# A DRAM buffer re-laid by head: one load over 96 partitions where there were six over 16

## The chip, the cores and the metric

The kernel runs on one core of one Trainium2 chip. The metric is the device time of one execution in microseconds (us), from the start of the program to its end. It does a whole transformer-like block for 32 batches of 512 tokens with hidden size 256: a token mixing, an attention with relative position terms, and a mixture of 8 experts.

## The reference, cut to what matters

The reference computes `h = tok(x)`, then `h = h + attn(layernorm(h))`, then `h = h + ffn(layernorm(h))`. The change touches only the attention's queries and keys:

```python
q = _split_heads(hidden_states @ Wq + bq, b, s)          # 16 heads of 16
k = _split_heads(hidden_states @ Wk + bk, b, s)
scores = jnp.einsum('bhqd,bhkd->bhqk', q, k) / scale
pos_k = (re @ Wpk + bpk) ...; pos_q = (re @ Wpq + bpq) ...
c2p = take_along_axis(einsum('bhqd,hpd->bhqp', q, pos_k), c2p_idx) / scale
p2c = swapaxes(take_along_axis(einsum('bhkd,hpd->bhkp', k, pos_q), p2c_idx)) / scale
probs = softmax(scores + c2p + p2c)
ctx = einsum('bhqk,bhkd->bhqd', probs, v); return ctx @ Wo + bo
```

## The kernel before, in words

The program runs in stages one after the other: a short table stage, `project`, `attend`, `output`, `choose`, `experts`. The change touches the DMA instructions of `project` and of `attend`, both issued by SyncE (SP).

**Splitting a number in three.** Queries and keys are float32, but the matmuls of the scores run in bfloat16. So `project` splits each value into three bfloat16 parts (high, middle, low), and the product of two such values is taken as six products of parts (`SLOTS = 6`, with `SIDE_A` and `SIDE_B` naming the part of each side). For one head of 16 features the contraction is therefore over `ST = 6 x 16 = 96` rows, and three more rows carry a term of the keys. These 99 rows are the `stack` of a head: 96 (or 99) partitions by `SW = 1280` columns, of which 512 are queries and 768 keys.

**project** (lines 313 to 634) works batch by batch, 32 times. In one batch TensorE mixes the tokens (`mixing`, line 394), turns the normalised rows, and makes queries, keys and values; ScalarE and GpSimd and VectorE keep and split them into `part_q` and `part_k`, tiles of 128 partitions (8 heads of 16 features), 2 halves `c` (heads 0 to 7 and 8 to 15) and 512 or 768 columns, three parts each. `part_q` and `part_k` have two buffers, `xt` (the input) has two, `v_sb` has one. SP's program for one batch `n`, in this order (lines 358 to 377): wait until the mixing of `n` has been done and load the input `xt` of batch `n + 2`; store `d_h`; wait for the values and store `d_v`; wait for all parts, and write them into `d_stack` in DRAM with 12 transfers (`for j in range(SLOTS)`, one of queries and one of keys each); write `d_kterm` with two. ScalarE waits for the writes of two batches ago before it fills `part_q` and `part_k` again, and for the `d_kterm` writes of the batch before.

**attend** (lines 636 to 1033) works head by head, 512 heads in all, numbered `n`; a loop runs over the batches and a Python `for` over their 16 heads. For head `n + 5` TensorE makes the position tables (`tables`, line 847) from `stack`, ScalarE keeps them in `skew_in`, and SP writes them to DRAM (`write_tables`, line 730) and reads them back, two heads later, at another pitch (`read_tables`, line 740), which is how the take-along-axis is done. GpSimd and VectorE finish the table of a head (`part`, `fill`), TensorE adds it to the head's scores in PSUM (`scores`, lines 860 to 867), VectorE moves the scores out, adds more table and takes the maximum (line 999), TensorE turns them (`turn`, line 876), ScalarE takes the exponent, and TensorE makes the context (line 889).

The stack of two heads (a group) is one buffer of a ring of `SR = 4`. SP loads group `k + 3` at head `2k`, after `read_tables(n + 3)` in program order: it waits until the scores of the group that had the buffer are done, and issues six loads of 16 partitions by 2 heads by 1280 columns from `d_stack` (line 714) and one of three partitions from `d_kterm` (line 717). After them come `write_tables(n + 5)`, and at some heads loads of the values (line 721) and a store of the context (line 746). TensorE needs the group for `tables` of head `2k + 6`, which it does during head `2k + 1`; its wait there is on all seven transfers (`STACKS = SLOTS + 1`), and everything that TensorE has behind it in program order waits too.

**output** (from line 1035) reads the context and the softmax sums back, with transfers whose DRAM side is `[8, 16, 512]` and whose SBUF side is 128 partitions (`load_inputs`, `load_shares`), and GpSimd multiplies them (line 1145).

Of the kernel before, what the change touches and what calls it, by code (L numbers as in the profile page):

```python
# [17 lines left out]
BF16 = mybir.dt.bfloat16  # L18
# [6 lines left out]
P = 128  # L25
S = 512
H = 256
ND = 4
NH = 16
HD = H // NH  # L30
QT = S // P
HC = H // P
# [17 lines left out]
SLOTS = 6  # L50
SIDE_A = (0, 0, 1, 0, 2, 1)
SIDE_B = (0, 1, 0, 2, 0, 1)
ST = SLOTS * HD
PLAIN = 3
KW = S + S // 2
SW = S + KW
# [4 lines left out]
SH = 2  # L61
# [10 lines left out]
def after(eng, sem, count):  # L72

    if not isinstance(count, int) or count > 0:
        eng.wait_ge(sem, count)  # L75


def settled(eng, sem, count, passed):


    after(eng, sem, count)
    if not isinstance(count, int):
        eng.sem_inc(passed, 1)  # L83


def peeled(eng, steps, body):

    body(0, steps == 1)
    if steps > 2:
        with eng.Fori(1, steps - 1, 1) as i:  # L90
            body(i, False)
    if steps > 1:
        body(steps - 1, True)


def build(nc, io, B):
    T = B * S
    NT = T // P
    with ExitStack() as top:
        def sem(name):  # L100
            return top.enter_context(nc.semaphore(name))

        def dram(name, shape, dt=F32):
            return nc.dram_tensor(name, shape, dt).ap()

        passed = sem("passed")
        d_tab = dram("d_tab", (2, 3, H, TW), BF16)
        d_stack = dram("d_stack", (B, SLOTS, H, SW), BF16)
        d_plain = dram("d_plain", (PLAIN, NH, TW), BF16)
        d_kterm = dram("d_kterm", (B, 3, NH, KW), BF16)  # L110
        d_v = dram("d_v", (B, S, NH * VROW))
        d_h = dram("d_h", (B, S, H))
        d_skew = dram("d_skew", (RING, P, PITCH))
        d_ctx = dram("d_ctx", (B, NG, P, S))
        d_share = dram("d_share", (B, NH, S))
        d_xg = dram("d_xg", (T, XG))
        d_scores = dram("d_scores", (P, NE, NT))
        d_floor = dram("d_floor", (P, 2))

        with ExitStack() as ctx:  # L120
            project(nc, io, B, ctx, sem, passed, d_tab, d_plain, d_stack, d_kterm, d_v, d_h)
        with ExitStack() as ctx:
            attend(nc, io, B, ctx, sem, passed, d_tab, d_plain, d_stack, d_kterm, d_v, d_skew, d_ctx)
        with ExitStack() as ctx:
            scores = ctx.enter_context(nc.sbuf_tensor("scores", [P, NE, NT], F32))
            with ExitStack() as inner:
                output(nc, io, B, inner, sem, passed, scores, d_h, d_ctx, d_share, d_xg)
            chosen = ctx.enter_context(nc.sbuf_tensor("chosen", [P, NE, CT], U32))

            w1, w2, b2 = (ctx.enter_context(nc.sbuf_tensor(name, shape, F32)) for name, shape in (  # L130
                ("w1", [P, 2, HC, DFF]), ("w2", [P, 2, FC, H]), ("b2", [P, 2, H])))
            w_in = [sem(f"e_w_in{u}") for u in range(2)]

            def load_expert(sp, e, u):
                sp.dma_start(w1[:, u], io["w1"][e].rearrange("(c p) f -> p c f", p=P)).then_inc(w_in[u], 16)
                sp.dma_start(w2[:, u], io["w2"][e].rearrange("(c p) o -> p c o", p=P)).then_inc(w_in[u], 16)
                sp.dma_start(b2[:, u], io["b2"][e].partition_broadcast(P)).then_inc(w_in[u], 16)

            with ExitStack() as inner:
                choose(nc, io, NT, inner, sem, passed, scores, chosen, d_scores, d_floor, load_expert)  # L140
            with ExitStack() as inner:
                experts(nc, io, T, inner, sem, passed, chosen, d_xg, w1, w2, b2, w_in, load_expert)


def project(nc, io, B, ctx, sem, passed, d_tab, d_plain, d_stack, d_kterm, d_v, d_h):
    def sb(name, shape, dt=F32):
        return ctx.enter_context(nc.sbuf_tensor("p_" + name, shape, dt))
# [17 lines left out]
    with ExitStack() as tctx:  # L165
# [47 lines left out]
        with nc.Block() as block:  # L213
            @block.sync
            def _(sp):
                for dst, src in loads:
                    sp.dma_start(dst[:], src).then_inc(t_in, 16)
                for u in range(2):

                    sp.dma_start(xt[:, u], xT[u].rearrange("d (c p) s -> p (d c) s", p=P)).then_inc(x_in[u], 16)  # L220
                sp.wait_ge(t_dve, 26)
                for w in range(2):
                    for c in range(HC):
                        sp.dma_start(d_tab[w, :, c * P:(c + 1) * P, :].rearrange("t p x -> p t x"),
                                     parts[:, w, c]).then_inc(t_out, 16)
                sp.dma_start(d_plain.rearrange("t h x -> h t x"), plain_parts[:]).then_inc(t_out, 16)
                sp.wait_ge(t_out, 16 * (2 * HC + 1))
# [104 lines left out]
    part_q = sb("part_q", [P, 2, 3, HC, S], BF16)  # L332
    part_k = sb("part_k", [P, 2, 3, HC, KW], BF16)
# [14 lines left out]
    h_out = [sem(f"p_h_out{u}") for u in range(2)]  # L348
    v_out, t_out = sem("p_v_out"), sem("p_t_out")
    parts_out = [sem(f"p_parts_out{u}") for u in range(2)]  # L350
    DMAS = 2 * SLOTS
    CH = 2 * HC
    pairs = B // 2

    with nc.Block() as block:
        @block.sync
        def _(sp):
            def body(i, last):
                for u in range(2):
                    n = 2 * i + u  # L360
                    if not last:
                        settled(sp, h_done, 2 * (n + 1), passed)
                        sp.dma_start(xt[:, u], xT[n + 2].rearrange("d (c p) s -> p (d c) s", p=P)
                                     ).then_inc(x_in[u], 16)
                    settled(sp, h_kept, 2 * (n + 1), passed)
                    sp.dma_start(d_h[n].rearrange("(t p) o -> p t o", p=P), h_sb[:, u]).then_inc(h_out[u], 16)
                    settled(sp, v_kept, 2 * (n + 1), passed)
                    sp.dma_start(d_v[n].rearrange("(t p) o -> p t o", p=P),
                                 v_sb[:].rearrange("p t h r -> p t (h r)")).then_inc(v_out, 16)
                    settled(sp, parts_done, (CH + 1) * (n + 1), passed)  # L370
                    for j in range(SLOTS):
                        to = d_stack[n, j].rearrange("(c p) x -> p c x", p=P)
                        sp.dma_start(to[:, :, 0:S], part_q[:, u, SIDE_A[j]]).then_inc(parts_out[u], 16)
                        sp.dma_start(to[:, :, S:SW], part_k[:, u, SIDE_B[j]]).then_inc(parts_out[u], 16)
                    to = d_kterm[n].rearrange("t h x -> h t x")
                    sp.dma_start(to[:, :, 0:S], part_t[0:NH]).then_inc(t_out, 16)
                    sp.dma_start(to[:, :, S:], part_t[NH:, :, 0:KW - S]).then_inc(t_out, 16)

            peeled(sp, pairs, body)
            sp.wait_ge(v_out, 16 * B)  # L380
            sp.wait_ge(t_out, 32 * B)
            for u in range(2):
                sp.wait_ge(parts_out[u], 16 * DMAS * pairs)
                sp.wait_ge(h_out[u], 16 * pairs)
# [75 lines left out]
        def _(act):  # L460
# [13 lines left out]
            def keep_qk(n, i, u, m):  # L474
                c = m % HC
                if m == 0:
                    after(act, parts_out[u], 16 * DMAS * i)
                if m == HC:
# [157 lines left out]
def attend(nc, io, B, ctx, sem, passed, d_tab, d_plain, d_stack, d_kterm, d_v, d_skew, d_ctx):  # L636
    def sb(name, shape, dt=F32):
        return ctx.enter_context(nc.sbuf_tensor("a_" + name, shape, dt))

    def ps(name, shape, dt=F32):  # L640
# [7 lines left out]
    stack = sb("stack", [ST + 3 + PLAIN, SR, SH, SW], BF16)  # L648
# [16 lines left out]
    stack_in = [sem(f"a_stack_in{u}") for u in range(SR)]  # L665
# [4 lines left out]
     pv_done, ctx_kept, ctx_out) = (sem("a_" + n) for n in (  # L670
         "tab_done", "tab_kept", "high_kept", "parted", "filled", "s_done", "s_kept", "lowered",
         "turn_done", "turned", "pv_done", "ctx_kept", "ctx_out"))
    STACKS = SLOTS + 1
    HEADS = B * NH
    PARTS = 5
    TURN = 2
# [21 lines left out]
    with nc.Block() as block:  # L698
        @block.sync
        def _(sp):  # L700
# [9 lines left out]

            def load_stack(b, g):
                u = g % SR
                for j in range(SLOTS):
                    sp.dma_start(stack[j * HD:(j + 1) * HD, u],
                                 d_stack[b, j, g * SH * HD:(g + 1) * SH * HD].rearrange("(h d) x -> d h x", d=HD)
                                 ).then_inc(stack_in[u], 16)
                sp.dma_start(stack[ST:ST + 3, u, :, S:], d_kterm[b, :, g * SH:(g + 1) * SH]
                             ).then_inc(stack_in[u], 16)

# [29 lines left out]
            for g in range(SR - 1):  # L749
                load_stack(0, g)  # L750
# [86 lines left out]
        def _(pe):  # L837
            def tables(n, b, hh, part):

                g, w, half = hh // SH, part % 2, part // 2  # L840
                if hh % SH == 0 and part == 0:
                    after(pe, stack_in[g % SR], 16 * STACKS * (NS // SR * b + g // SR + 1))
                after(pe, tab_kept, 4 * n + part - 1)
# [862 lines left out]
```

## Time and profile before

| | |
|---|---|
| Time, median of 3 runs | 5799.73 us (5794.48 to 5809.27) |
| The profiled execution, its time | 5817.07 us |
| Its span in the trace | 5815.3 us |
| TensorE busy | 4793.1 us (82%) |
| VectorE busy | 3453.9 us (59%) |
| ScalarE busy | 2652.2 us (46%) |
| GpSimd busy | 1528.6 us (26%) |
| Moved by DMA | 1543.71 MB, mean 265 GB/s |
| Packets of SP's DMA queue, share of the 16 DMA engines' span | 78.8% |

The stages can be told apart by their lines: `project` runs to 982 us (the last `d_stack` write is issued at 977.4 us), `attend` from there to about 4910 us, `output` to about 5320 us, the experts after it. Most of the time is `attend`. A share of busy time is a mean over all stages, so each stage has to be read by itself.

### The profile page before, as it was taken

To read this page: it belongs to the slowest core of one execution; us is meant where nothing else is said; L and a number is where in the kernel's file an instruction comes from. 1 tells how busy PE (TensorE), PEld (TensorE's weight loads), DVE (VectorE), ACT (ScalarE), POOL (GpSimd) and SP (SyncE) were. 2 spreads that over 40 slices of the span, in tenths; PEclk is the share of its full clock that TensorE was granted. 3 is DMA by queue.
4 is the path that set the end of the run, shared out by engine and by line. 5 is a ranking of instruction groups with operands and counts; after the bars stand their busy time and mean duration, and the time that the engine had idled before them with its cause. 6 is when DMAs were issued, how large, how long until landed. Compare 5 with 4: busy or idle time off the path is not lost. (4 is left out here: it accounts for less than half of the span.)

```text
span 5815.3 us, 116776 instructions
## 1 busy us (share of the span) xinstructions
PE 4793.1 (82%) x31272; PEld 3401.2 (58%) x31272; DVE 3453.9 (59%) x9058; ACT 2652.2 (46%) x4937; POOL 1528.6 (26%) x3442
## 2 busy tenths in 40 slices
PE   6999996788888888888888888888888888774588
PEld 5666664555555655555556555555555555563455
DVE  3344443666666666666667666666666666676611
ACT  1333332555555555555555555555555555010011
POOL 1222232222222222222222222222222222452022
PEclk9999998899999999999999999999999999786589
DMA  4777777999988999998899989999899897674033
GB/s 157 258 254 248 256 258 225 317 313 305 308 299 294 307 310 305 303 311 300 299 309 308 316 296 307 306 304 301 299 305 314 297 301 250 226 253 144 2 78 74
DMA packets 682097, 1543.71 MB, mean 265 GB/s; under 512 B 59715, under 2 KB 300275, under 8 KB 681587
## 3 DMA queue, kind: packets, MB, share of 16 engines
q1 hardware_dynamic: 675446, 1528.58, 78.8%
q0 software_dynamic: 6144, 8.52, 0.9%
q8 instruction: 300, 4.92, 0.4%
q14 instruction: 207, 1.70, 0.1%
HBM read 762.99 MB, written 773.87 MB: 264 GB/s over the span
## 5 line engine op out<-in xcount | busy, mean ns | idle before, releaser
L999 DVE CUSTOM_DVE_ANT_1 a_scored<-a_ps_m_s,a_bias 128x512 f32<-128x512 f32 x2048 | 1398.8, 683 | 1264.7 <-PE a_ps_m_s L867 1238.8
L936 ACT ACTIVATE a_probsT<-a_ps_m_t 128x512 f32<-128x512 f32 x2048 | 1225.7, 605 | 1255.4 <-PE a_ps_m_t L876 1253.1
L815 POOL TENSOR_SCALAR_AFFINE_SELECT a_bias<-a_bias 128x128 f32<-128x128 f32 (+2 forms) x2560 | 903.9, 381 | 2877.8 <-DMA a_bias<-d_skew 2796.8
L930 ACT ACTIVATE a_skew_in<-a_ps_m_tab 128x512 f32<-128x512 f32 x2048 | 1119.4, 608 | 453.7 <-PE a_ps_m_tab L847 392.3
L876 PE MATMUL a_ps_m_t<-a_ident,a_scored 128*128 128x128 f32 x8192 | 1311.3, 285 | 0.5 <-ACT a_probsT L936 0.5
L876 PEld LDWEIGHTS a_ps_m_t<-a_ident,a_scored 128*128 128x128 f32 x8192 | 978.4, 146 | 457.4 <-DVE a_scored L1006 380.2
L847 PE MATMUL a_ps_m_tab<-a_tabs,a_stack 96*128 96x256 bf16 (+1 forms) x4096 | 728.8, 291 | 464.9 <-DMA a_stack<-d_kterm 445.3
L1006 DVE TENSOR_SCALAR a_scored<-a_scored,a_top_of 128x512 f32<-128x512 f32 x2048 | 964.9, 492 | 0.0
L867 PE MATMUL a_ps_m_s<-a_ident,a_bias 128*128 128x128 f32 x5120 | 943.0, 283 | 0.0
L862 PE MATMUL a_ps_m_s<-a_stack 99*128 99x512 bf16 (+2 forms) x2048 | 728.0, 355 | 198.9 <-issue 147.2
L867 PEld LDWEIGHTS a_ps_m_s<-a_ident,a_bias 128*128 128x128 f32 x5120 | 712.9, 148 | 121.9 <-issue 15.4
L847 PEld LDWEIGHTS a_ps_m_tab<-a_tabs,a_stack 96*128 96x128 bf16 (+1 forms) x4096 | 361.8, 103 | 665.0 <-issue 467.1
L889 PE MATMUL a_ps_m_ctx<-a_probsT,a_values 128*17 128x512 f32 x4096 | 563.2, 623 | 1.2 <-ACT a_ctx_sb L942 1.2
L984 DVE COPY_PREDICATED a_bias<-a_ps_m_past,a_high 128x384 f32<-128x384 int32 x1024 | 544.5, 586 | 32.4 <-POOL a_high L801 32.4
L394 PE MATMUL p_ps_m_h<-p_mix,p_xt 128*128 128x256 f32 x2048 | 467.1, 382 | 7.3 <-PEq L213 7.3
L394 PEld LDWEIGHTS p_ps_m_h<-p_mix,p_xt 128*128 128x128 f32 x2048 | 389.9, 192 | 99.6 <-issue 51.9
L862 PEld LDWEIGHTS a_ps_m_s<-a_stack 99*128 99x128 bf16 x2048 | 206.5, 101 | 315.0 <-issue 242.6
L860 PE MATMUL a_ps_m_s<-a_stack 99*128 99x128 bf16 (+1 forms) x1024 | 263.1, 257 | 0.0
L1179 PE MATMUL o_ps_m_o<-o_wo,o_ctxn 128*128 128x256 f32 x512 | 169.3, 503 | 65.3 <-POOL o_ctxn L1145 65.3
L1179 PEld LDWEIGHTS o_ps_m_o<-o_wo,o_ctxn 128*128 128x128 f32 x512 | 130.6, 261 | 94.9 <-POOL o_ctxn L1145 37.2
L539 POOL TENSOR_TENSOR p_rest_q<-p_full_q,p_part_q 128x512 f32<-128x512 f32 x64 | 90.3, 1411 | 330.8 <-ACT p_part_q L486 330.8
L539 POOL TENSOR_TENSOR p_rest_k<-p_full_k,p_part_k 128x768 f32<-128x768 f32 x64 | 105.1, 1643 | 241.5 <-ACT p_part_k L491 241.5
(182 smaller groups left out, 3631.1 us busy)
## 6 DMA issues: line engine op xcount, KB each, us to landing
d_skew<-a_skew_in SPq DMA_DIRECT2D x512, 1024.0 KB, 5.9
a_bias<-d_skew SPq DMA_DIRECT2D x512, 896.0 KB, 7.9
a_stack<-d_stack SPq DMA_DIRECT2D x1536, 80.0 KB
d_stack<-p_part_k SPq DMA_DIRECT2D x192, 384.0 KB, 3.8
p_xt<-in_xT SPq DMA_DIRECT2D x32, 2048.0 KB, 9.4
d_stack<-p_part_q SPq DMA_DIRECT2D x192, 256.0 KB, 3.5
d_ctx<-a_ctx_sb SPq DMA_DIRECT2D x128, 256.0 KB, 6.9
d_v<-p_v_sb SPq DMA_DIRECT2D x32, 544.0 KB, 3.0
```

The source lines that it names most:

```text
L394: mm = pe.matmul(m_h[:, t], xt[:, u, k, t * P:(t + 1) * P], mix[:, k], start=(k == 0), stop=(k == ND * HC - 1))
L815: nc.gpsimd.affine_select(blocks(r + out[0], (out[1], count)), blocks(r + of, (2, count)), pattern=[[0, count], [-sign, P]], base=0, chann ...
L847: mm = pe.matmul(m_tab[:, w, k], stack[0:rows, g % SR, hh % SH, at:at + P], tabs[0:rows, w, hh], start=True, stop=True)
L862: pe.matmul(bank[:, far:], q, row[:, S + far:2 * S], start=not far, stop=False, skip_group_check=True)
L867: mm = pe.matmul(bank[:, k * P:(k + 1) * P], bias[:, at], ident[:], start=False, stop=(k == near[-1]), is_transpose=True, skip_group_check ...
L876: mm = pe.transpose(m_t[:, k % 2, t * P:(t + 1) * P], scored[:, hh % SCORED, t, k * P:(k + 1) * P], ident[:])
L889: mm = pe.matmul(m_ctx[j * CROW:j * CROW + VROW], values[:, half, k, (g * GH + j) % (NH // 2)], turned_at(g, j, k), start=(k == 0), stop=( ...
L930: nc.scalar.activation(skew_in[:, u, w, 2 * half:2 * half + 2], m_tab[:, w], ACT.Identity).then_inc(tab_kept, 1)
L936: nc.scalar.activation(turned_at(hh // GH, hh % GH, k), m_t[:, k % 2], ACT.Exp, scale=SCALE).then_inc(turned, 1)
L984: nc.vector.copy_predicated(blocks(r + at, (step, QT - 1)), m_past[:, w].unsqueeze(1).to_broadcast([P, QT - 1, P]), high[:, v, w].unsqueez ...
L999: nc.vector.tensor_tensor_reduce(split(scored[:, hh % SCORED, t]), split(m_s[:, t % 2]), extra, 1.0, -3.0e38, ALU.add, ALU.max, top_of[:, ...
L1006: nc.vector.tensor_scalar(at, at, top_of[:, hh % 2, t:t + 1], None, ALU.subtract).then_inc(lowered, 1)
```

## The change

In DRAM the stack was laid out `(batch, slot, feature row of all heads, column)`. Now it is laid out `(batch, head, row of the head's 96, column)`. The load of a group becomes one transfer over 96 partitions; the three-row load from `d_kterm` stays, so the wait counts two transfers where it counted seven. The writes in `project` must now say which head a row belongs to, so each covers one half `c` of the heads, and there are 24 per batch where there were 12. The bytes are the same in both directions. The ring keeps its four buffers.

```diff
-        d_stack = dram("d_stack", (B, SLOTS, H, SW), BF16)
+        d_stack = dram("d_stack", (B, NH, ST, SW), BF16)
@@ project
-    DMAS = 2 * SLOTS
+    DMAS = 2 * SLOTS * HC
@@
                     for j in range(SLOTS):
-                        to = d_stack[n, j].rearrange("(c p) x -> p c x", p=P)
-                        sp.dma_start(to[:, :, 0:S], part_q[:, u, SIDE_A[j]]).then_inc(parts_out[u], 16)
-                        sp.dma_start(to[:, :, S:SW], part_k[:, u, SIDE_B[j]]).then_inc(parts_out[u], 16)
+                        for c in range(HC):
+                            to = d_stack[n, c * NH // HC:(c + 1) * NH // HC, j * HD:(j + 1) * HD]
+                            sp.dma_start(to[:, :, 0:S], part_q[:, u, SIDE_A[j], c]).then_inc(parts_out[u], 16)
+                            sp.dma_start(to[:, :, S:SW], part_k[:, u, SIDE_B[j], c]).then_inc(parts_out[u], 16)
@@ attend
-    STACKS = SLOTS + 1
+    STACKS = 2
@@
             def load_stack(b, g):
                 u = g % SR
-                for j in range(SLOTS):
-                    sp.dma_start(stack[j * HD:(j + 1) * HD, u],
-                                 d_stack[b, j, g * SH * HD:(g + 1) * SH * HD].rearrange("(h d) x -> d h x", d=HD)
-                                 ).then_inc(stack_in[u], 16)
+                sp.dma_start(stack[0:ST, u], d_stack[b, g * SH:(g + 1) * SH].rearrange("h r x -> r h x")
+                             ).then_inc(stack_in[u], 16)
                 sp.dma_start(stack[ST:ST + 3, u, :, S:], d_kterm[b, :, g * SH:(g + 1) * SH]
                              ).then_inc(stack_in[u], 16)
```

Before, the two sides of a write were `[128, 2, 512]` on both sides; now the DRAM side is `[8, 16, 512]` (8 heads, 16 rows of each) and the SBUF side `[128, 512]`.

## Rows read from the trace of the kernel before

**Rows 1.** Windows of project, attend, output: busy us (instructions) by engine, clock, DMA.

```profile
core 0: us, PE busy (x) PEld busy (x) DVE busy (x) ACT busy (x) POOL busy (x), PEclk, DMA share, GB/s
150.00:900.00 750.00, 726.29 (x2873) 509.73 (x2872) 305.14 (x696) 252.82 (x450) 219.28 (x160) 1.00 0.76 254
1100.00:4800.00 3700.00, 3116.19 (x23258) 2175.59 (x23256) 2487.64 (x6786) 2131.32 (x3998) 943.05 (x2905) 0.94 0.92 305
5000.00:5300.00 300.00, 235.72 (x1147) 198.51 (x1148) 230.06 (x607) 38.13 (x87) 159.88 (x85) 0.82 0.72 246
```

**Rows 2.** Waits of PE, 1050:4950: us in total, times, longest.

```profile
PE a_ps_m_tab L847 <- DMA a_stack<-d_kterm: 402.7, 221, 4.2
PE a_ps_m_s L862 <- issue: 147.2, 29, 5.6
```

**Rows 3.** Timeline of SP in attend, heads 2k, 2k+1, 2k+2: start, duration.

```profile
3072.35 0.52 SPq L740 DMA_DIRECT2D a_bias<-d_skew  x1
3073.12 2.92 SPq L714 DMA_DIRECT2D a_stack<-d_stack  x6
3076.22 0.25 SPq L717 DMA_DIRECT2D a_stack<-d_kterm  x1
3078.76 0.52 SPq L740 DMA_DIRECT2D a_bias<-d_skew  x1
...
3086.35 0.79 SPq L740 DMA_DIRECT2D a_bias<-d_skew  x1
```

**Rows 4.** Timeline of PE in the same heads, in brackets the idle time before.

```profile
3081.24 0.61 PE L847 MATMUL a_ps_m_tab<-a_tabs,a_stack 96*128 96x256 bf16 x4 [1.28 <-DMA a_stack<-d_kterm]
```

**Rows 5.** Source view of the table reads of all 512 heads, line 740.

```profile
L740 SPq DMA_DIRECT2D a_bias<-d_skew x512: 518/524/1736, 1015.7 to 4897.4; - x171
```

**Rows 6.** Windows of 4 us: stack load flowing, not flowing, after a long stall.

```profile
3076.00:3080.00 4.00, 3.91 (x31) 2.34 (x29) 4.00 (x12) 2.10 (x4) 0.16 (x1) 1.00 1.06 281
3080.00:3084.00 4.00, 2.76 (x24) 2.41 (x25) 1.47 (x6) 2.79 (x6) 1.67 (x6) 1.00 1.02 388
3104.00:3108.00 4.00, 4.00 (x18) 1.69 (x17) 0.70 (x2) 0.30 (x1) 0.00 (x0) 0.50 0.88 234
```

**Rows 7.** Timeline of PE and SP at the start of attend.

```profile
993.75 2.66 SPq L714 DMA_DIRECT2D a_stack<-d_stack  x6
...
1002.91 1.01 PE L847 MATMUL a_ps_m_tab<-a_tabs,a_stack 96*128 96x256 bf16 x4 [37.31 <-DMA a_stack<-d_kterm]
```

**Rows 8.** Timeline of SP in one batch of project.

```profile
410.85 0.37 SPq L368 DMA_DIRECT2D d_v<-p_v_sb  x1
413.36 0.37 SPq L373 DMA_DIRECT2D d_stack<-p_part_q  x1
...
419.45 0.58 SPq L373 DMA_DIRECT2D d_stack<-p_part_q  x1
...
421.29 0.58 SPq L373 DMA_DIRECT2D d_stack<-p_part_q  x1
...
423.13 0.59 SPq L376 DMA_DIRECT2D d_kterm<-p_part_t  x1
...
426.15 0.38 SPq L366 DMA_DIRECT2D d_h<-p_h_sb  x1
439.12 0.37 SPq L368 DMA_DIRECT2D d_v<-p_v_sb  x1
```

**Rows 9.** View of transfers: count, KB each, median us to landing where known.

```profile
d_skew<-a_skew_in SPq DMA_DIRECT2D x512, 1024.0 KB, 5.9
...
d_stack<-p_part_k SPq DMA_DIRECT2D x192, 384.0 KB, 3.8
p_xt<-in_xT SPq DMA_DIRECT2D x32, 2048.0 KB, 9.4
d_stack<-p_part_q SPq DMA_DIRECT2D x192, 256.0 KB, 3.5
...
o_shares<-d_share SPq DMA_DIRECT2D x64, 256.0 KB
...
d_floor<-c_pair SPq DMA_DIRECT2D x1, 1.0 KB, 2.7
```

**Rows 10.** Waits of POOL in output, 5000:5300.

```profile
POOL o_ctxn L1145 <- DMA o_shares<-d_share: 128.2, 28, 5.2
```

**Rows 11.** The page's line on packets.

```profile
DMA packets 682097, 1543.71 MB, mean 265 GB/s; under 512 B 59715, under 2 KB 300275, under 8 KB 681587
```

## The prediction

> **What bounds the kernel now.** I read the windows by stage first [rows 1]. In project TensorE is busy 726 of 750 us: the stage is bound by TensorE, with the DMA engines at a share of 0.76. In attend TensorE is busy 84% at a clock of 0.94, VectorE 67%, and the DMA share is 0.92: nothing is full, but DMA is nearest. So I read the waits next [rows 2]. TensorE waits for the stack of a group 221 times in some 240 groups, 402.7 us, mean 1.82 us. The other wait, 147.2 us in 29, comes once per turn of the batch loop; the change doesn't touch it. Third, the timeline shows why the stack is late. SP begins the head by issuing the table read at 3072.35, then needs from 3073.12 to 3076.47 for the seven loads [rows 3], and the tables start at 3081.24, after a wait of 1.28 us [rows 4]: 8.89 us from the trigger, where TensorE could have used the data at 7.61. SP's next heads show the price: 6.41 us for the head without such a wait (3072.35 to 3078.76), 7.59 for the one with it (3078.76 to 3086.35) [rows 3]; the mean over 512 heads is 3881.7 / 511 = 7.60 us [rows 5]. In attend the chain is thus: scores of the old group, SP's issue, transfer, tables, all that TensorE has behind them.
>
> **Attend: issue time.** Six loads and their gaps take 3.10 us of SP (3073.12 to 3076.22) [rows 3]. The one load over 96 partitions has 192 runs of 2560 B. The trace has no such load; the six now take 0.49 us each for 32 runs, and the table read takes 0.52 us for 256 runs [rows 3], so the count of runs hardly enters: I take 0.55, bounds 0.3 and 1.3 (if the queue holds SP back for the 1.3 us in which 480 KB pass at 388 GB/s [rows 6]). SP gains 2.5 us per group. That is more than the mean wait of 1.82.
>
> **Attend: the transfer.** In the 4 us in which the stack load flows, the share is 1.06 but only 281 GB/s move; in the next 4 us it is 1.02 at 388 GB/s [rows 6]. So the same engines, as busy, moved 0.43 MB less, which is 1.1 us at 388 GB/s. I read it as the price of loads that land in only 16 partitions at a time; over 96 partitions it should go, but the window also holds a mixture of reads and writes, so bounds are 0 and 1.1 us per group.
>
> **Attend: the sum.** Upper bound: all waits go (403 us), and the clock comes back. At a clock of 0.94 the 3116 us of TensorE are 187 us longer than at full clock [rows 1]; a window at 0.50 follows a stall of the batch loop [rows 6], and those stay, so at most about 100 of it: 500 us. Lower bound: the DMA share is 0.92 already [rows 1], so the stage gains only what the engines save, and of that half: 0.55 x 256 = 140 us. Heads that follow faster ask more of the queue: at 7.60 us per head 305 GB/s, at 6.4 us 362, against the 388 of an undisturbed window. So a part of the wait must return, in the stack or in the table reads. I take 1.1 us per group, 256 x 1.1 = 282 us, which is 70% of the wait and equals what the engines save at an unchanged share. At the start three groups are loaded one after the other behind a TensorE that waits 37.31 us [rows 7]: three times 2 us less, 6 us. Attend: -288.
>
> **Project: twelve more writes, and narrower ones.** SP issues 24 instead of 12. It stood idle from 426.53 to 439.12, 12.6 us per batch [rows 8], so issue alone would be hidden. The question is how wide the new writes run. Their DRAM side is `[8, 16, 512]`. The output stage has transfers of just that shape: per batch two of `o_c_in` and two of `o_shares`, 256 KB each [rows 9]. There GpSimd waits for them in each of its 28 batches, although the DMA share is only 0.72 at 246 GB/s [rows 1, 10]. That fits engines of which one half is full and the other isn't. Per batch (10.7 us) the 1024 KB of this shape over 8 engines are 128 KB each, the other 1552 KB (`h`, `out`, `xg`) over 16 are 97 KB: the lower half would carry 225 KB, the upper 97, a mean share of (1 + 0.43) / 2 = 0.72, as seen. So I charge the new writes to 8 engines.
>
> Rule against trace: the Trainium skill ("DMA: Bandwidth & Descriptors", section "Why a DMA increments its semaphore by 16 and not by 1") says that a copy is split over the largest count up to 16 that divides the slowest dimension of both sides, and that each engine used posts one completion. By that rule 3,933 transfers in the view (its first and last line in [rows 9]) would post 62,928 small packets, less 13 x 256 for the three-partition loads and 8 x 128 for the two output kinds; with 1,152 short runs of small constants that is 59,728, and the page counts 59,715 under 512 B [rows 11]. The trace agrees, and by the rule the writes here use 8 engines; a split by the 128 partitions would leave project at no change.
>
> Now the sum. Stack writes per batch: 6 x (256 + 384) KB = 3.93 MB [rows 9]. All of a batch: 254 GB/s x 28.27 us = 7.18 MB [rows 1, 8], so 3.25 MB is the rest. The lower half carries 3.93 / 8 + 3.25 / 16 = 0.695 MB per engine. One engine's pace is 254 / (0.76 x 16) = 20.9 GB/s [rows 1], or by the steady part of the writes (a pair every 1.84 us, 655 KB, 356 GB/s [rows 8]) 22.3. That gives 33.2 or 31.2 us per batch; I take 32.4 (between the two), so +4.1 over 28.27. The bound below is 0 (an engine that reaches 388 / 16 = 24.3 GB/s [rows 6] needs 28.7), the bound above is rival B. The input load is issued 12 us later and needs 9.4 us [rows 9], but has two buffers, some 31 us per batch, and doesn't decide. 31 periods x 4.1 = 127, and the last batch's writes, for which attend waits, end 12 us later (9.8 us of issue from 413.36 to 423.13 [rows 8] become 12 x 1.84 = 22): 139 us.
>
> **Net.** 5817 - 288 + 139 = 5668 for the profiled execution; it lies 17 us above the median of the runs, so I predict 5651, 2.6% faster.
>
> **Rivals.**
> A. The wait only moves. DMA stays at 0.92 and the table reads become late in place of the stack: GpSimd waits, then TensorE's scores. For it: the share; against it: windows of 388 GB/s. Attend -140, project +139: 5799, no change.
> B. Slower. The narrow writes are not only a matter of engine load: SP is held by the full queue for the whole longer write, 24 writes at the pace of 8 engines take 22 us, and `d_kterm`, the input load and `d_h` stand behind them. If all of the extra 12.3 us is on the path of every batch (the input load late, TensorE without work), project costs 31 x 12.3 = 381, with the end 393, and attend gives 288: 5905. It decides from (288 - 12) / 31 = 8.9 us per batch on. For it: the idle time of SP is 12.6 us, just the extra; against it: the two input buffers.
> C. The writes run on all 16 engines (the split follows the 128 partitions). Project 0, attend -288: 5512. Against it: output's share.
> D. All of the wait goes and the clock rises: attend -440, project +139: 5499. For it: heads of 6.4 us [rows 3].
>
> **Chances.** Forecast 0.44, A 0.17, B 0.15, C 0.09, D 0.15. The forecast's own range, with attend -200 to -360 and project +70 to +190, is 5550 to 5770. Over all cases 5480 to 5830 leaves out most of B and little else. What a measurement can tell from no change is 0.3%, 17 us. Of A a third is faster, a third the same, a third slower; some of B is within reach of no change. Faster 0.75, same 0.07, slower 0.18.
>
> **What would show it.** In project: batch period about 32 us between stores of `d_v`, TensorE near 85%, the DMA share near 0.75 with fewer GB/s (about 222), and input or buffer waits of TensorE where there are none. An unchanged 28.3 would prove C. In attend: one L714 of about 0.5 us per group, the wait of L847 on the stack from 403 to about 100 us, heads of 7.0 us in the mean (line 740, first to last, some 3600 us), more than 320 GB/s. If the stack's wait goes but heads stay at 7.4 with new waits of the scores or of GpSimd, it is A. The prediction fails if project grows by more than 9 us a batch, or if attend gains less than 140.

## The result, and the profile after

The changed kernel takes 5836.94 us (median of 5 runs, 5822.52 to 5846.09), the kernel before 5796.51 us on the same chip. The ratio is 1.0064 with a 95% interval of 1.0042 to 1.0087: 0.6% slower. The forecast was 5651 us with a range of 5480 to 5830.

The first view of the changed kernel is the windows by stage, as in [rows 1]; attend starts later now, so its window is 1200 to 4900.

```profile
core 0: us, PE busy (x) PEld busy (x) DVE busy (x) ACT busy (x) POOL busy (x), PEclk, DMA share, GB/s
150.00:900.00 750.00, 659.95 (x2508) 463.65 (x2507) 268.62 (x602) 220.78 (x396) 195.49 (x139) 0.95 0.65 220
1200.00:4900.00 3700.00, 3185.02 (x24032) 2221.01 (x24031) 2564.68 (x7013) 2200.08 (x4131) 970.91 (x3002) 0.95 0.92 315
```

Project moves 220 GB/s where it moved 254, and TensorE's work in the same 750 us fell from 726 to 660 us. Attend moves 315 GB/s where it moved 305, at an unchanged share of 0.92.

The source view gives the length of each stage: first and last start of the `d_v` stores (project) and of the table reads (attend), and for these the time from issue to landing.

```profile
L368 SPq DMA_DIRECT2D d_v<-p_v_sb x32: 372/372/509, 102.2 to 1101.8; - x32
L739 SPq DMA_DIRECT2D a_bias<-d_skew x512: 518/530/1341, 1163.4 to 4926.8; - x171
...
DMA to landing us min/median/max: 5.0/7.7/11.7
```

Project: 999.6 / 31 = 32.25 us per batch (predicted 32.4; by the same row of before, 100.5 to 966.4, it was 27.93). Attend: 3763.4 / 511 = 7.36 us per head where it was 7.60 [rows 5]. The first table read comes 147.7 us later than before and the last one 29.4 us later, so attend gained 118 us and the stages ahead of it lost 148. The two spans differ by 29.1 us: nothing else moved.

The SP timeline in project shows where the time goes: the stores of `d_v` of four batches.

```profile
361.17 0.37 SPq L368 DMA_DIRECT2D d_v<-p_v_sb  x1
389.36 0.37 SPq L368 DMA_DIRECT2D d_v<-p_v_sb  x1
426.49 0.37 SPq L368 DMA_DIRECT2D d_v<-p_v_sb  x1
454.68 0.37 SPq L368 DMA_DIRECT2D d_v<-p_v_sb  x1
```

Batches take 28.2, 37.1 and 28.2 us in turn: the old period, then one with a stall. The waits of PE and of ACT in project (150 to 1125 us) name the stall; each comes in every second batch.

```profile
PE p_ps_m_h L395 <- DMA p_xt<-in_xT: 87.7, 16, 7.4
...
ACT p_full_t L500 <- DMA d_kterm<-p_part_t: 94.7, 16, 14.0
```

Both transfers stand behind the 24 writes in SP's program. In attend, the waits of PE from 1200 to 4950 us, which answer to [rows 2]:

```profile
PE a_ps_m_tab L846 <- DMA a_stack<-d_kterm: 311.3, 215, 3.3
PE a_ps_m_s L861 <- issue: 151.2, 29, 5.8
```

The wait on the stack, whose loss was to bring the gain, is still there in 215 groups, 1.45 us each in place of 1.82. The timeline of SP and of PE around one of them answers to [rows 3, 4].

```profile
3094.36 0.37 SPq L729 DMA_DIRECT2D d_skew<-a_skew_in  x1
3096.16 0.53 SPq L739 DMA_DIRECT2D a_bias<-d_skew  x1
3096.94 0.64 SPq L714 DMA_DIRECT2D a_stack<-d_stack  x1
3097.76 0.29 SPq L716 DMA_DIRECT2D a_stack<-d_kterm  x1
```

```profile
3104.81 0.61 PE L846 MATMUL a_ps_m_tab<-a_tabs,a_stack 96*128 96x256 bf16 x4 [1.36 <-DMA a_stack<-d_kterm]
```

SP has issued the stack 1.89 us after the start of the table read (3098.05) where it took 4.12 before. But the tables start 8.65 us after the table read was issued, where it was 8.89. From the end of SP's issue to the tables it was 4.77 us and is now 6.76: what SP gained was lost again between issue and landing. Ahead of the stack in SP's queue (the transfers in the order in which SP issued them) stand the 1024 KB of the table write and the 896 KB of the table read, and this read alone takes 7.7 us from issue to landing in the median, more than the 7.29 us after which TensorE wants the stack. That it is this, the packet records of the traces and the experiments show.

A packet of a stack load has 2560 B and one of a table read 3584 B, so the records tell when each load flows. For groups 20 to 239, in the median: in the changed kernel the first packet of a stack load starts 3.75 us after the load's issue, and the last one ends 1.50 us after the last packet of the table read ahead of it (80% of the groups lie between 1.20 and 1.85). In the kernel before this last figure was 1.55 us. So the load ends close behind the read ahead of it.

### The profile page after: what moved, and what is told of

The parts are those of the page before. It is cut to its first block and busy times, and to the rows that moved or that the text cites. A ratio compares the mean times of both kernels' runs of the same rounds, so it can differ in the third digit from the quotient of the medians.

```text
span 5844.4 us, 114151 instructions
## 1 busy us (share of the span) xinstructions
PE 4792.2 (82%) x31271; PEld 3394.1 (58%) x31272; DVE 3456.1 (59%) x9058; ACT 2647.3 (45%) x4937; POOL 1528.7 (26%) x3442
## 2 busy tenths in 40 slices
DMA packets 661617, 1543.63 MB, mean 264 GB/s; under 512 B 39235, under 2 KB 279795, under 8 KB 661107
## 5 line engine op out<-in xcount | busy, mean ns | idle before, releaser
L395 PE MATMUL p_ps_m_h<-p_mix,p_xt 128*128 128x256 f32 x2048 | 500.4, 401 | 100.7 <-DMA p_xt<-in_xT 93.4
L395 PEld LDWEIGHTS p_ps_m_h<-p_mix,p_xt 128*128 128x128 f32 x2048 | 413.2, 203 | 205.3 <-issue 142.2
L603 DVE CAST p_part_q<-p_rest_q 128x512 bf16<-128x512 f32 x64 | 27.3, 427 | 312.3 <-POOL p_rest_q L540 312.3
```

Source lines behind the costliest of these rows:

```text
L395: mm = pe.matmul(m_h[:, t], xt[:, u, k, t * P:(t + 1) * P], mix[:, k], start=(k == 0), stop=(k == ND * HC - 1))
```

## The experiments

All ratios are to the kernel before on the same chip. The experiments ran on several chips, on which the kernel before took 5777 to 5797 us, so kernels are compared by their ratios and not by their microseconds. "Per head" is the first to the last table read over 511, from one profiled execution. Diffs are cut, and `@@` stands where lines are left out (constants, closing lines).

**1. Wide writes with the same load.** A third layout, one row per feature with the six slots of it side by side. It leaves the 12 writes 128 wide on both sides and still gives one load over 96 partitions, since slot and feature have one common step. The rows of `stack` and `tabs` are then ordered by feature, then slot.

```diff
-        d_stack = dram("d_stack", (B, SLOTS, H, SW), BF16)
+        d_stack = dram("d_stack", (B, H, SLOTS, SW), BF16)
@@
-                        to = d_stack[n, j].rearrange("(c p) x -> p c x", p=P)
+                        to = d_stack[n, :, j].rearrange("(c p) x -> p c x", p=P)
@@
-                    sp.dma_start(tabs[j * HD:(j + 1) * HD, w],
+                    sp.dma_start(tabs[j:ST:SLOTS, w],
@@
+                sp.dma_start(stack[0:ST, u],
+                             d_stack[b, g * SH * HD:(g + 1) * SH * HD].rearrange("(h d) j x -> (d j) h x", d=HD)
@@
```

> Third layout: d_stack is (batch, feature row, slot, column), so that the 12 writes of a batch stay 128 partitions wide on both sides and the load is still one over 96 partitions (the rows of stack and tabs are ordered by feature, then slot). Theory W (the whole cost in project is the width of 8): project returns to a period of 28.3 us per batch and attend stays as in the changed kernel (7.37 us per head): 5837 - 31 x 4.0 - 12 = 5700 us, 1.7% below before. Theory I (the cost in project came from elsewhere in the new layout, such as DRAM rows further apart, or the gain in attend needs rows that lie together): project stays near 32 us or attend goes back to 7.6, 5800 or more.

Measured: 5662.99 us, ratio 0.9796 (0.9768 to 0.9824). The `d_v` stores run from 98.8 to 967.9, 28.04 us per batch, and heads take 7.31 us. Theory W holds: the cost in project goes with the width of the writes, all but 0.1 us a batch of it (28.04 against 27.93), and from 150 to 1125 us neither PE's wait for the input nor ACT's for `d_kterm` is left.

**2. 24 writes, all wide.** The kernel before, each write cut in two halves of 128 rows.

```diff
-    DMAS = 2 * SLOTS
+    DMAS = 2 * SLOTS * HC
@@
+                        for c in range(HC):
+                            to = d_stack[n, j, c * P:(c + 1) * P]
+                            sp.dma_start(to[:, 0:S], part_q[:, u, SIDE_A[j], c]).then_inc(parts_out[u], 16)
+                            sp.dma_start(to[:, S:SW], part_k[:, u, SIDE_B[j], c]).then_inc(parts_out[u], 16)
```

> The kernel before with its 12 writes per batch cut into 24 by halves, each with 128 rows on both sides, the layout unchanged. Theory W: the number of issues is hidden by SP's 12.6 us of idle time per batch and the engines carry the same bytes: period 28.3 us, the time of before within 0.3% (5797). Theory N (the number of transfers costs): period above 29.5 us, 5835 or more.

Measured: 5777.44 us, ratio 1.0003 (0.9987 to 1.002). The number of writes costs nothing; the period of `project` is 27.93 us as before. The packet records show the width as well. In the parts of `project` in which only packets of the stack writes move (150 to 900 us), 16 of them are in flight in the median before and in this run, and 8 in the changed kernel.

**3. The load ahead of the table read.** The changed kernel, two blocks of SP's program exchanged.

```diff
+                    if hh % SH == 0:
+                        g = hh // SH + SR - 1
+                        if not (last and g >= NS):
+                            settled(sp, s_done, QT * n, passed)
+                            load_stack(b + g // NS, g % NS)
                     if not (last and hh + NEXT >= NH):
                         m = hh + NEXT
                         read_tables(n + NEXT, b + m // NH, m % NH)
-                    if hh % SH == 0:
-                        g = hh // SH + SR - 1
-                        if not (last and g >= NS):
-                            settled(sp, s_done, QT * n, passed)
-                            load_stack(b + g // NS, g % NS)
```

> The changed kernel, with the load of the stack issued ahead of the table read of the same head instead of behind it. Theory Q (what is left of the stack wait, 315 us in 216 waits, is time in the DMA queue behind the 896 KB table read): the stack lands some 2.3 us earlier, the wait falls below 100 us, the table reads land 1.3 us later where they have slack, attend gains 150 us or more: 5680. Theory C (the stage is bound by what the DMA engines carry at a share of 0.91): the wait moves to the table reads or the scores and the time stays within 30 us of 5837.

Measured: 5488.47 us, ratio 0.9499 (0.9474 to 0.9524): 5.6% less than the changed kernel. The window of attend (1200 to 4400), the waits of PE and the source view of its table reads:

```profile
1200.00:4400.00 3200.00, 2949.58 (x22852) 2053.92 (x22850) 2447.40 (x6667) 2060.37 (x3929) 940.20 (x2866) 0.97 0.98 347
```

```profile
PE a_ps_m_tab L846 <- DMA a_stack<-d_kterm: 15.7, 30, 2.4
```

```profile
L739 SPq DMA_DIRECT2D a_bias<-d_skew x512: 518/532/1473, 1160.5 to 4571.2; - x171
...
DMA to landing us min/median/max: 4.8/8.2/12.2
```

The wait is nearly gone (30 waits, 15.7 us), heads take 6.67 us, and the table reads, which now land 0.5 us later (8.2 against 7.7 us), have the slack for it. Theory Q holds, by much more than the 150 us that it gave as its least: attend, from the first to the last table read, takes 353 us less than in the changed kernel, whose TensorE waited 311 us for the stack. The granted clock of attend is 0.97 here and was 0.95 there. DMA went to 347 GB/s at a share of 0.98, so the 0.92 of before was no ceiling.

**4. A ring of eight groups** in the changed kernel (`SR = 8` in place of 4).

> The changed kernel with a ring of eight groups, SR = 8, so that each load is issued four groups earlier than it is needed. No wait on the stack can be left. It prices that wait: theory Q gives attend -315 us and some 50 for the clock, 5480 us, heads of 6.7 us; theory C (the DMA engines are the bound) gives at most 2 or 3% of attend, 5740 us, with new waits on the table reads.

Measured: 5480.42 us, ratio 0.9483 (0.9456 to 0.951), heads of 6.64 us, and from 1200 to 4400 us no wait on the stack among PE's waits. The order alone (experiment 3) reaches within 0.2% of it, with half of the buffers.

**5. Issue time by itself.** The changed kernel with five tiny loads ahead of each load of the stack, which hold SP and carry next to nothing.

```diff
+                settled(sp, pad_in, 16 * (SLOTS - 1) * before, passed)
+                for k in range(SLOTS - 1):
+                    sp.dma_start(pad[:, k], d_kterm[0, :, 0, k * 64:(k + 1) * 64]).then_inc(pad_in, 16)
                 sp.dma_start(stack[0:ST, u], d_stack[b, g * SH:(g + 1) * SH].rearrange("h r x -> r h x")
```

> The changed kernel, with five tiny loads (three partitions by 128 B, never read) ahead of each load of the stack: SP issues the stack some 2.3 us later, as late as the kernel before finished its six, but the load keeps its 96 partitions. It prices the term of issue time alone, for which the prediction took most of attend's gain. Theory Q (the load stands behind the table read in the DMA queue anyway, so most of an earlier issue is waited out there): under a third of 2.3 us a group comes back, at most 256 x 0.8 = 200 us and rather 60, ratio to before 1.01 to 1.02. Theory P (the issue is on the chain in full, as predicted): 256 x 2.3 = 590 us less what the wait's slack takes, ratio 1.07 or more.

```profile
3093.90 0.52 SPq L744 DMA_DIRECT2D a_bias<-d_skew  x1
3094.68 1.81 SPq L718 DMA_DIRECT2D a_pad<-d_kterm  x5
3096.67 0.35 SPq L719 DMA_DIRECT2D a_stack<-d_stack  x1
```

```profile
PE a_ps_m_tab L852 <- DMA a_stack<-d_kterm: 250.7, 187, 3.4
```

Measured: 5811.87 us, ratio 1.0065 (1.0042 to 1.0089), heads of 7.27 us. SP issues the stack 1.99 us later (3094.68 to 3096.67, its timeline above), and the ratio is that of the changed kernel, 1.0064. The wait on the stack (the second fence, 1200 to 4400 us: 250.7 us in 187) is that of the changed kernel too (267.1 us in 185). The packets say why: the first one of a stack load now starts 1.76 us after the issue instead of 3.75, and the last one again ends 1.52 us after the table read's last. Behind the table read, the issue time that the change saves is worth nothing; that is less than even theory Q gave it (1.01 to 1.02).

**6. The same event, only the place differs.** In experiment 3 the load also goes out earlier by the clock, since it waits for scores done and the table read for scores kept. Here it waits for the same as the table read. The edit is shown against the kernel of experiment 3.

```diff
-                            settled(sp, s_done, QT * n, passed)
+                            settled(sp, s_kept, QT * n, passed)
                             load_stack(b + g // NS, g % NS)
```

> The changed kernel with the stack's load ahead of the table read, as in the run that gave 5488 us, but waiting for the same event as the table read does (the last scores kept, not only done), so that it is not issued any earlier than SP's turn of before; only its place in the queue differs from the changed kernel. If the place is the cause, the ratio to before is that of the load first (0.950) within 0.01. If the earlier trigger (some 1.2 us) was the cause, it goes back towards 1.006, to 0.98 or more.

Measured: 5524.29 us, ratio 0.9529 (0.9513 to 0.9545). PE waits for the stack 60 times from 1200 to 4400 us, 47.1 us in all. The place in the queue carries the gain; the earlier trigger adds 0.3%, which is no more than the two intervals allow for. The load is still issued up to 0.8 us earlier than in the changed kernel, since the issue of the read no longer comes before it, but by experiment 5 a shift of 2 us in the issue counts for nothing as long as the place stays.

**7. Six narrow loads again**, in the changed kernel and its layout.

```diff
-                sp.dma_start(stack[0:ST, u], d_stack[b, g * SH:(g + 1) * SH].rearrange("h r x -> r h x")
+                for j in range(SLOTS):
+                    sp.dma_start(stack[j * HD:(j + 1) * HD, u],
+                                 d_stack[b, g * SH:(g + 1) * SH, j * HD:(j + 1) * HD].rearrange("h r x -> r h x")
@@
```

> The changed kernel and its layout by head, but with the load cut into six over 16 partitions again. It splits the 118 us that attend gained. If they come from the load's shape, heads go back to 7.6 us and the time is 5837 + 118 = 5955. If they come from the layout in DRAM (rows of a head together), it stays at 5837.

Measured: 5918.51 us, ratio 1.024 (1.0197 to 1.0283), heads of 7.51 us. That is 1.7% over the changed kernel: most of attend's gain came from the shape of the load (its issue, which the cut makes longer too, counts for nothing here by experiment 5). The 5955 of the first theory was not quite reached; the last 0.09 us per head may be the layout or scatter, since attend of experiment 2, the same code as before, took 7.53 where before took 7.60.

**8. The kernel before with a ring of eight.**

> The kernel before with a ring of eight groups, so that no wait on the stack is left while the loads stay six over 16 partitions. It prices the shape of the load by itself, against the changed kernel with a ring of eight (heads of 6.64 us). If the shape costs the engines 0.6 to 1.1 us per group, as read before, heads take 6.9 to 7.2 us and the time is 5797 - 512 x 0.5 = 5540 us (5450 to 5590). If the shape costs nothing, heads take 6.65 us and the time is 5340.

Measured: 5433.95 us, ratio 0.9397 (0.9359 to 0.9435), heads of 6.81 us. Its window (1200 to 4400):

```profile
1200.00:4400.00 3200.00, 2891.32 (x22366) 2010.11 (x22366) 2436.58 (x6525) 2022.41 (x3843) 956.16 (x2796) 0.97 1.00 340
```

Without any stack wait the narrow loads run the DMA engines at a share of 1.00 for 340 GB/s; the wide one needs 0.99 for 348 (experiment 10). The difference in the time of a group, (6.81 - 6.64) x 2 = 0.35 us, is the price of the shape. The times agree: against the ring of eight in the third layout (experiment 10), which differs from this run only in the layout and its one load, the ratios 0.9397 and 0.9232 are 96 us apart, 0.37 us per group. I expected 0.6 to 1.1 and a time of 5450 to 5590, or 5340 if the shape cost nothing; it came out between the two.

**9. The kernel before, its six loads first** (the exchange of experiment 3).

> The kernel before, its six loads of 16 partitions kept, only moved ahead of the table read. Theory Q (order in the queue is what matters): the stack lands some 2 us earlier and the wait of 400 us falls below 150; the table read is issued 3.3 us later and keeps its slack: 5797 - 200 = 5600 or faster. Theory S (the shape of the load matters as much): the six loads hold SP for 3.1 us and the engines for longer, so the table reads come late, the time stays within 60 us of before.

Measured: 5498.43 us, ratio 0.9509 (0.947 to 0.9548), heads of 6.98 us; the stack wait of attend is 161.0 us in 114 waits where it was 402.7 in 221, a little over the 150 that theory Q named. So one moved block in the kernel before gives 4.9%, with no new layout at all.

**10. Both findings together.** The third layout, once with the load first and once with a ring of eight.

> The third layout (wide writes, one load) with the load of the stack ahead of the table read. Both findings together, if they are independent: the changed kernel with the load first (5488 us, its project 137 us too long by the narrow writes) less 137 = 5351 us, ratio 0.926 to before. A rival says they are not independent, because attend with the load first runs the DMA engines at a share of 0.98 and rows laid 15 KB apart in DRAM could cost there: above 5400.

> The third layout with a ring of eight groups, the load behind the table read. With the load first the DMA engines run at a share near 0.98. If that is the bound, a deeper ring gives nothing beyond the order: the time of the third layout with the load first (5337 us, ratio 0.923) within 15 us. If stack waits still cost there, it is faster by more.

Measured: load first 5336.91 us, ratio 0.9232 (0.9194 to 0.927); ring of eight 5332.66 us, ratio 0.9232 (0.9214 to 0.925). Their source views and windows of attend, the load first and then the ring:

```profile
L739 SPq DMA_DIRECT2D a_bias<-d_skew x512: 518/529/1176, 1011.1 to 4423.3; - x171
```

```profile
1200.00:4400.00 3200.00, 2950.05 (x22854) 2053.45 (x22852) 2447.20 (x6666) 2060.33 (x3929) 937.38 (x2856) 0.97 0.98 346
```

```profile
1200.00:4400.00 3200.00, 2960.78 (x22984) 2062.57 (x22977) 2495.32 (x6702) 2072.03 (x3950) 974.12 (x2880) 0.97 0.99 348
```

The parts add up (a ratio of 0.926 expected, 0.923 measured), and a deeper ring brings no more than the order. In this order the one wide load is worth something: the six narrow loads in the same place (experiment 9) keep 161.0 us of stack waits, take 6.98 us per head where this takes 6.68, and give 0.9509 against 0.9232. At a share of 0.98 to 0.99 and TensorE at 92% of the window, both are near full. This is the fastest version found, 7.7% below before.

## Why the prediction was wrong

**What bounds the kernel now: half right.** The stack wait was the right wait, and it was worth about what rival D gave it (440 us): with a ring of eight heads take 6.81 us with the narrow loads (401 us less over attend) and 6.64 with the wide one (489 less). But the chain was drawn as SP's issue, transfer, tables, with the issue as a free term. Between issue and transfer stands the queue.

**Attend, issue time: the step that failed.** "SP gains 2.5 us per group. That is more than the mean wait of 1.82." The first half came true (2.23 us in the heads compared above). The second half took a gain in issue for a gain in landing. The stack's load stands in SP's queue behind the table read, which itself takes 7.7 us to land, while TensorE wants the stack after 7.29 (the heads above); an issue in no time at all would have left a wait. By the packets the load ends 1.5 us after the read, in the changed kernel and in experiment 5, 2 us of issue apart. The trace of before could have told this: the 4.77 us from SP's last issue to the tables were in [rows 3, 4], more than the 3.5 to 3.8 us in which the writes of project land [rows 9], and I did not ask why. Experiment 5 puts 2.0 of SP's microseconds back and nothing changes. Experiments 3 and 6 leave the load as it is and change the place, experiment 6 with the trigger of the table read, and nearly all of the wait goes. The size of the whole term: 288 us predicted for attend, 118 measured, plus 3 at its start. That is below the 140 which the prediction had named as its own sign of failing, and it puts the time above the range.

**Attend, the transfer: right in kind, too large.** The price of loads into 16 partitions was read as 0 to 1.1 us per group. Without stack waits it is 0.35 us (experiments 8 and 10); behind the table read, experiment 7 gives (7.51 - 7.36) x 2 = 0.28 by the heads and 0.40 by the ratios (0.0176 x 5797 / 256). The 4 us windows of [rows 6] also differed in their mixture of reads and writes, as the text allowed, and I should have weighed that more.

**Attend, the sum: wrong for a second reason.** The 1.1 us per group was called the part that the DMA share of 0.92 [rows 1] would allow. The share was not a limit: the stage went to 0.98 and 347 GB/s as soon as the wait had gone. So rival A named the right outcome (the time about unchanged, the wait still felt) by a wrong mechanism: the table reads never became late, and the stack's own wait stayed.

**Project: right, but for the input load.** Period 32.25 against 32.4 (the middle of two estimates, 31.2 and 33.2, so its closeness is in part luck), the stores of `d_v` 134 us further apart from first to last, and from the last one to the first stack load 16 us more (27.3 before, from 966.4 to 993.75 [rows 7]; 43.1 after, from 1101.8 to 1144.9): 149 in all against 139. The charge of the new writes to 8 engines, taken from the output stage, is confirmed in four ways. The mean share with one half full follows from the bytes, 0.695 MB and 0.203 MB per engine: (1 + 0.29) / 2 = 0.65, which is the row; the prediction's "near 0.75" did not follow from its own figures. Experiments 1 and 2 give the time back with wide writes and lose none with many. The packets in flight are 8 where they were 16 (experiment 2). And the page's packets under 512 B fall from 59715 [rows 11] to 39235:

```profile
DMA packets 661617, 1543.63 MB, mean 264 GB/s; under 512 B 39235, under 2 KB 279795, under 8 KB 661107
```

The difference, 20480, is 5 x 256 x 16, the loads that went. The 384 additional writes added none: 768 x 8 is 384 x 16. This agrees with the rule of the Trainium skill ("DMA: Bandwidth & Descriptors", section "Why a DMA increments its semaphore by 16 and not by 1").

What I had put aside is that the input load "has two buffers and doesn't decide". It does appear, as the 37.1 us batch after a 28.2 us one: TensorE's waits for it are 87.7 us of the 134 that project lost. It comes late because it stands behind the 24 slow writes, so its cause is again their width (experiment 1). Whether the pair's mean is set by the full half of the engines, as the sum has it, or by this chain, no run separates.

**Rival B** had its mechanism in part (input load and `d_kterm` late behind the writes, both seen in the waits) at a third of its price: 4.3 us per batch, not 12.3. Rival C is excluded. What decided the sign was not project but the gain that attend did not give.

## What to carry to other kernels

When a consumer waits for a transfer, look at what stands ahead of it in the same DMA queue before counting how long its issue takes: here one exchange of two blocks was worth 4.9% in the kernel before, 5.6% in the changed one and 5.8% in the third layout, and 2 us less of issue nothing. When a layout is changed for the reader's sake, write down the outermost count of both sides of the writer's transfers too; here a count of 8 halved the engines, and a third layout with one common step served both. A DMA share of 0.92 beside a regular wait was no ceiling here: remove the wait in an experiment (a deeper ring) and see where the share goes.

## What was not expected of the hardware

A write of 128 runs on 8 engines holds SP for at least 0.593 us, where one of 256 runs on 16 engines took 0.372 at best; the source views of the query writes:

```profile
L374 SPq DMA_DIRECT2D d_stack<-p_part_q x384: 593/625/1412, 104.7 to 1126.0; - x192
```

Before, the same writes had 372/574/1917 (min, median, max, ns). The 24 wide writes of experiment 2 have the bytes and the 128 runs of the narrow ones, on 16 engines:

```profile
L374 SPq DMA_DIRECT2D d_stack<-p_part_q x384: 332/332/460, 105.6 to 982.1; - x192
```

So the smaller size makes SP's issue shorter, and the width of 8, or the `[8, 16, 512]` shape of the DRAM side that brings it, makes it longer: 0.625 us in the median on 8 engines, 0.332 on 16. No run separates the shape from the width. And the share of the DMA engines reaches 1.00 over 3.2 ms (experiment 8) while TensorE is busy 90% of the same time: in this stage the one does not keep the other from being nearly full.
